# Reordering the first attention layer of a fused attention and FFN kernel: scores behind the values, row maxima turned in a projection bank, normalised rows made on ScalarE

## The chip, the cores and the metric

The kernel runs on one core of a Trainium2 chip. The metric is device time in microseconds of one execution; the result is compared as the median of several runs. The engines are TensorE (PE, with its weight loads as PEld), VectorE (DVE), ScalarE (ACT), GpSimd (POOL) and SyncE (SP), which here only issues DMAs. Each engine carries out its own list of instructions in order; semaphores order them against each other.

## The reference

The program is two transformer-like layers over `x` of 32 batches x 128 rows x 128 columns, with a context of 77 rows per batch. The change touches only the first attention:

```python
x = x + _L0_xattn_ref(_layernorm(x), ctx, ctx, Wq, Wk, Wv, Wo, mask)
# inside: 16 heads of 64, rope on Q and K
Q = (q @ Wq).reshape(b, ql, 16, 64); K = (k @ Wk)...; V = (v @ Wv)...
Q, K = rope(Q), rope(K)
attn = einsum('bqhd,bkhd->bhqk', Q / 8, K)
attn = where(mask == 0, -INF, attn); attn = softmax(attn)
out = einsum('bhqk,bkhd->bqhd', attn, V) @ Wo
```

Then come an FFN, a second attention (16 heads of 8) and a second FFN, each with its layer norm. The mask is given for each batch (128 x 77 int32).

## The kernel before

The first attention goes batch by batch; one batch is a **slot** `b` (0 to 31), two batches are a **pair** `p`, and slot `b` is even (`j == 0`) or odd (`j == 1`) in it. Every engine has a function `slot`, in which its work for a batch is written out by hand; nothing else sets the order. A slot holds work of several batches at once:

- TensorE, for batch `b`: `all_scores` (transposed scores of all heads, 32 small matmuls, L1274, and 16 "fold" matmuls, L1278, which add the mask and subtract each row's maximum), later `values` (L1296), `turn_maxima` (one transpose of the maxima of batch `b + 1`, L1244), `turn_out` (8 transposes of the normalised output, L1307) and `out_projection` (L1316). The fold matmuls read the tile `fold`, which ScalarE copies from the turned maxima (`fold_in`, L1057).
- TensorE, for later batches: `score_maxima(b + 1)` (bf16 scores with the mask, L1223 and L1232, from which VectorE takes each row's maximum, `maxima`, L911), and projections, each three matmuls per piece (`split_product`, L1172 to L1174): four of queries (Q) in each even slot, for the next pair; keys (K tasks, 8 for each group of 4 batches, 308 columns) by the table `KEYS`; values (V, two halves of 512 columns for a tile of 128 context rows) by `VALUE_SLOT`; and the transposes of the next normalised rows (X, L1164, L1167) in each odd slot.
- Rope: VectorE multiplies a projection by the cosines (L845 for Q, L855 for K) and swaps lanes (L848, L858), which frees the projection's bank; GpSimd multiplies the swapped part by the sines and adds (L741 and L742 for Q, L753 and L755 for K). ScalarE casts the results to bf16 (`cast_queries`, L1045; `cast_keys`, L1053), exponentiates the scores (`exps`, L1062 and L1067), copies V out of its bank (`values_in`, L1040) and the turned output (`turned_out`, L1073).
- Layer norm rows: VectorE takes statistics (`statistics`, L806 to L812) in an even slot, GpSimd the power (`pre`, L729), and VectorE in the odd slot makes the mask tile `am` (L801), `kept` (L802), `scale` (L817) and the normalised rows `xhat` (L819).

Two PSUM banks, `pa[0]` and `pa[1]`, take all projections in turn. The list `pa_tasks` names every such task in order; task number `i` uses bank `i % 2`, and TensorE may start it only when task `i - 2` has been read out:

```python
    for i, name in enumerate(pa_tasks()):
        TASK[name] = (i % 2, count[i % 2])
    def empty(engine, name):
        engine.wait_ge(a_free[TASK[name][0]], TASK[name][1])
```

A fourth bank of scores ("S") is one of these tasks; the turned maxima are not, they lie in the score bank `ps[0]`. `cast_keys(b)` waits for all keys that batch `b` may need:

```python
    def keys_of(b):
        return 4 + 4 * (b // 2) if b < 4 else 8 + 8 * (b // 4)
            act.wait_ge(k_roped, keys_roped(keys_of(b)))
```

so batch 2 needs keys 0 to 7, and keys 4 to 7 are made in slot 0. The masks come by DMA into two buffers, `mask_in[p % 2]`; SyncE loads that of pair `p + 2` when the X task of pair `p` has been read.

## Time and profile before

| | us |
|---|---|
| median of 3 runs (717.77 to 719.16) | 718.37 |
| the profiled execution | 719.26 |
| its span in the trace | 716.7 |
| TensorE busy in the span | 680.4 (95%) |
| slots 2 to 31 of the first attention, in the trace | about 64 to 444 |

Times in the trace count from the start of the span. A matmul is drawn with its whole latency, so that neighbours overlap: what it really occupies is the distance from its start to the start of the next. A short wait is therefore not seen as idle time but as a larger distance of two starts.

### The profile page before, as it was taken

How to read it: one execution, taken by the hardware profiler on the slowest of the kernel's cores; microseconds unless marked ns; L12 is line 12 of the kernel's file. 1: busy time of each engine (PE TensorE's matmuls, PEld its weight loads, DVE VectorE, ACT ScalarE, POOL GpSimd, SP SyncE). 2: the span in 40 equal slices, each digit the busy share in tenths (PEclk: the TensorE clock that was granted, in tenths of full speed). 3: DMA queues.
4: the chain of work that ended last, by engine and by line, in shares of the span. 5: the costliest groups of instructions: out<-in, count | busy, mean ns of one | idle time of the engine just before them, and what ended most of it. 6: DMA issues, size and time to landing. Idle time of an engine off the chain costs nothing.

```text
span 716.7 us, 23519 instructions
## 1 busy us (share of the span) xinstructions
PE 680.4 (95%) x9268; PEld 569.8 (80%) x9273; DVE 556.9 (78%) x1635; ACT 388.7 (54%) x846; POOL 432.1 (60%) x558
## 2 busy tenths in 40 slices
PE   8999999999999999999999989999999999998875
PEld 6788888888888888889888878788888888875544
DVE  5887787697687698688687655787878887778996
ACT  2443553543544544445345444566766766766896
POOL 3597586487396388378477523455555646632775
PEclk9999999999999999999999999999999999998999
DMA  9511011101101101101100120000000000000011
GB/s 263 132 34 37 13 48 45 33 5 46 37 26 45 36 2 45 36 26 36 36 22 15 32 79 7 11 7 7 12 5 4 9 4 9 0 2 1 24 45 52
DMA packets 26766, 23.82 MB, mean 33 GB/s; under 512 B 7148, under 2 KB 23356, under 8 KB 26680
## 3 DMA queue, kind: packets, MB, share of 16 engines
q1 hardware_dynamic: 25864, 22.25, 11.1%
q8 instruction: 62, 1.02, 0.6%
q10 hardware_dynamic: 816, 0.36, 0.2%
q14 instruction: 24, 0.20, 0.1%
HBM read 10.25 MB, written 2.10 MB: 17 GB/s over the span
## 4 chain that ended last, share of the span: by engine, by line
PE 70%; DVE 17%; POOL 5%; issue 4%; ACT 3%; DMA 1%; SPq 0%; ACTq 0%; DVEq 0%
PE bank L1274 7%; PE bank L1316 6%; PE bank L1942 6%; PE bank L1172 5%; PE bank L1296 4%; PE bank L1975 4%; PE bank L1278 4%; PE bank L1307 3%; PE bank L1173 3%; PE bank L1174 3%; DVE a_am L911 3%; PE bank L1960 2%; DVE f_h_max L2192 2%; PE bank L1223 2%; PE bank L1232 2%
## 5 line engine op out<-in xcount | busy, mean ns | idle before, releaser
L741 POOL TENSOR_TENSOR a_turned<-a_turned,a_rope 128x512 f32<-128x512 f32 x63 | 81.7, 1297 | 55.7 <-DVE a_turned L848 55.7
L742 POOL TENSOR_TENSOR a_qr<-a_straight,a_turned 128x512 f32<-128x512 f32 x64 | 81.6, 1276 | 4.9
L845 DVE TENSOR_TENSOR a_straight<-bank,a_rope 128x512 f32<-128x512 f32 x63 | 43.0, 683 | 52.5 <-PE bank L1174 51.4
L1045 ACT CAST a_qb<-a_qr 128x512 bf16<-128x512 f32 x64 | 39.8, 622 | 65.9 <-POOL a_qr L742 65.9
L1296 PE MATMUL bank<-a_vs,a_probs 77*64 77x65 f32 x2048 | 66.8, 222 | 0.0
L1296 PEld LDWEIGHTS bank<-a_vs,a_probs 77*64 77x64 f32 x2048 | 62.6, 137 | 3.3
L753 POOL TENSOR_TENSOR a_k_turned<-a_k_turned,a_rope 128x308 f32<-128x308 f32 x61 | 48.4, 793 | 24.3 <-DVE a_k_turned L858 23.6
L1316 PE MATMUL bank<-a_wo,a_oTn 128*128 128x128 f32 x512 | 62.6, 275 | 0.2 <-ACT a_oTn L1073 0.2
L1316 PEld LDWEIGHTS bank<-a_wo,a_oTn 128*128 128x128 f32 x512 | 60.5, 192 | 1.2 <-ACT a_oTn L1073 0.5
L911 DVE TENSOR_REDUCE a_am<-bank 128x6 bf16<-128x462 f32 (+1 forms) x96 | 49.9, 576 | 12.1 <-PE bank L1232 12.0
L1274 PE MATMUL bank<-a_qr,a_kr 64*77 64x128 f32 x960 | 59.2, 273 | 0.0
L1057 ACT COPY a_fold<-bank 112x128 bf16<-112x128 bf16 x32 | 8.5, 266 | 92.4 <-PE bank L1244 92.4
L1067 ACT ACTIVATE a_probs<-bank 77x512 f32<-77x512 f32 x98 | 52.8, 593 | 7.5 <-PE bank L1258 7.5
L1274 PEld LDWEIGHTS bank<-a_qr,a_kr 64*77 64x77 f32 x960 | 52.3, 144 | 5.2 <-issue 5.1
L755 POOL TENSOR_TENSOR a_kr<-a_k_straight,a_k_turned 128x308 f32<-128x308 f32 x62 | 52.0, 840 | 4.8
L848 DVE STREAM_SHUFFLE a_turned<-bank 128x512 f32<-128x512 f32 x63 | 46.3, 735 | 0.0
L1674 DVE TENSOR_REDUCE a_max_m<-bank 128x8 f32<-128x512 f32 x64 | 41.1, 685 | 5.0 <-PE bank L1923 4.6
L1812 ACT ACTIVATE a_qr<-bank 128x512 f32<-128x512 f32 (+1 forms) x96 | 43.8, 536 | 1.0 <-PE bank L1960 1.0
L729 POOL TENSOR_TENSOR a_rstd<-a_var,minus_half 128x2 f32<-128x2 f32 x16 | 11.3, 707 | 51.1 <-DVE a_var L812 51.0
L1073 ACT COPY a_oTn<-bank 128x512 f32<-128x512 f32 x64 | 34.5, 589 | 13.4 <-PE bank L1307 12.8
L1172 PE MATMUL bank<-a_xT_hi,a_wq_hi 128*128 128x256 f32 x128 | 39.9, 312 | 1.3 <-DVE a_wq_lo L939 1.1
L1599 POOL TENSOR_TENSOR a_kr<-a_k_straight,a_blocks 128x128 f32<-128x128 f32 x32 | 12.8, 400 | 46.4 <-ACT a_k_straight L1794 46.4
(282 smaller groups left out, 1984.8 us busy)
## 6 DMA issues: line engine op xcount, KB each, us to landing
a_vs<-a_stage SPq DMA_DIRECT2D x16, 312.8 KB
out<-x_all SPq DMA_DIRECT2D x16, 128.0 KB, 1.8
x_all<-in_x_dram SPq DMA_DIRECT2D x7, 256.0 KB, 6.3
a_vs<-a_stage SPq DMA_DIRECT2D x4, 308.8 KB
a_mask_in<-in_mask SPq DMA_DIRECT2D x16, 77.0 KB, 5.7
a_wv<-in_ctx SPq DMA_DIRECT2D x16, 77.0 KB
a_ctx_in<-in_ctx SPq DMA_DIRECT2D x8, 128.0 KB
a_vs<-a_stage SPq DMA_DIRECT2D x4, 211.2 KB
```

The lines of the kernel that those rows point to most:

```text
L741: steps.link(nc.gpsimd.tensor_tensor(tv, tv, rope[:, 1:2, :].broadcast_to([128, 4, S]), ALU.mult))
L742: nc.gpsimd.tensor_tensor(qr[P][:, 2 * k:2 * k + 2, :, :].rearrange("p t j s -> p (t j) s"), sv, tv, ALU.subtract if made else ALU.add).th ...
L753: steps.link(nc.gpsimd.tensor_tensor(tv, tv, rope[:, 3:4, 0:KL].broadcast_to([128, 4, KL]), ALU.mult))
L755: nc.gpsimd.tensor_tensor(kr[q % 2][:, lo:hi, first:end, :].rearrange("p i j s -> p i (j s)"), view(k_straight[n % 3]), view(k_turned[n % ...
L848: nc.vector.stream_shuffle(turned[k % 3][:], pv, mask=[lane ^ 1 for lane in range(32)]).then_inc(a_free[TASK["Q", p, k][0]], 1)
L911: nc.vector.tensor_reduce(rows, ps[bk][:, 0:n * KL].rearrange("p (h k) -> p h k", k=KL), AX, ALU.max).then_inc(s_free[bk], 1)
L1067: nc.scalar.activation(probs[:, 4 * g:4 * g + 4, :], ps[ST_BANK[g]][0:KL, :].rearrange("p (h s) -> p h s", s=S), ACT.Exp).then_inc(s_free[ ...
L1172: nc.tensor.matmul(out, lhs_hi, rhs_hi, start=True, stop=False)
L1274: nc.tensor.matmul(banks[g][0:KL, i * S:(i + 1) * S], kr[b // 4 % 2][e:e + 64, h // 2, b % 4, :], qr[P][e:e + 64, h // 2, j, :], start=i = ...
L1296: last = nc.tensor.matmul(po[r][rows, VW * i:VW * (i + 1)], probs[:, PROBS_SLOT[h], rows], vs[b % RING][:, h, :], start=True, stop=True)
L1316: last = nc.tensor.matmul(po[2][:, 0:D], oTn[:, i, :], wo[:, i, :], start=i == 0, stop=i == TILES - 1)
L1812: nc.scalar.activation(probs[:, 4 * g:4 * g + n, :], SCORES[g].rearrange("p (t s) -> p t s", s=S), ACT.Exp).then_inc(s_free[g], 1)
```

## The change

What each engine does in a slot is written in a new order, for slots 0 to 29; slots 30 and 31 keep theirs.

- TensorE: `all_scores(b + 1)` (only the 32 score matmuls) is issued directly behind `values(b)`, then `turn_maxima(b + 1)`, then `turn_out(b)`. The 16 fold matmuls of `all_scores` become `all_folds`, the first thing of the next slot.
- The turned maxima are a task of their own ("T") in the two projection banks, ahead of "S" in the list.
- Keys and values are spread otherwise over the slots: keys `lead` come directly behind the folds; an even slot from 4 to 26 has one key there (before, its one or two keys stood behind the score maxima and behind the values), an odd slot `4q + 1` six (before five).
- ScalarE makes the normalised rows (two passes over two batches, in the even slot), which VectorE made in the odd slot; GpSimd makes `scale`; VectorE gets `kept` straight from `mask_in`, in `statistics` of the even slot.
- ScalarE casts the keys of `b + 1` and of `b + 2` in the even slot (before, those of `b + 1` in each slot) and the queries two and two; `turned_out(b)` moves to the end of slot `b`.
- SyncE loads the mask of a pair when `am` of the pair before last has been made.

The core of the diff (lines as long as they are; "..." where left out):

```diff
-    VALUE_SLOT = {8 * o + s: VT * o + i for o in range(B // 8) for i, s in enumerate((-3, 0 if o == 0 else -1, 1, 3, 4))
-                  if 8 * o + s >= 0}
+    VALUE_SLOT = {0: (1,), **{8 * o + 1: (VT * o + 2,) for o in range(B // 8)}, **{8 * o + 3: (VT * o + 3,) for o in range(B // 8)},
+                  **{8 * o + 5: (VT * o + 4,) for o in range(B // 8)},
+                  **{8 * o - 1: (VT * o, VT * o + 1) for o in range(1, B // 8)}}
...
-    KEYS, LATE_KEYS = {0: range(4, 8), 1: range(8, 11), 2: range(14, 16)}, {1: range(11, 14)}
+    KEYS = {0: ((), (), range(4, 6), range(6, 8)), 1: (range(8, 9), range(9, 10), range(10, 12), range(12, 14)),
+            2: (range(14, 16), (), (), ())}
     for q in range(1, B // 4 - 1):
         n = 8 + 8 * q
-        KEYS[4 * q], KEYS[4 * q + 1], LATE_KEYS[4 * q + 1] = range(n, n + 2), range(n + 2, n + 5), range(n + 5, n + 7)
-        KEYS[4 * q + 2] = range(n + 7, n + 8)
...
+        KEYS[4 * q] = (range(n, n + 1), (), (), ())
+        KEYS[4 * q + 1] = (range(n + 1, n + 2), range(n + 2, n + 3), range(n + 3, n + 5), range(n + 5, n + 7))
+        KEYS[4 * q + 2] = (range(n + 7, n + 8), (), (), ())
...
+                    + [("V", 0, 1), ("C",), ("X", 1), ("T", 0), ("S", 0)])
...
+                yield from lead + queries[:2] + middle + queries[2:3] + first_half + second_half + queries[3:] + late
             else:
-                yield from values[:1] + rows + values[1:]
+                rows = [("X", p + 2)] if p + 2 < PAIRS else []
+                yield from lead + first_half + second + second_half + middle + later_first + rows + later_second + late
+            if b + 1 < B - 2:
+                yield "T", b + 1
+                yield "S", b + 1
...
-            if j == 0 and more_pre(p):
-
-                read(sp, ("X", p))
-                load_mask(p + 2)
+            if b == 0 or j == 1 and more_pre(p + 1):
+                at = 0 if j == 0 else p + 1
+                sp.wait_ge(masks_made, at + 1)
+                load_mask(at + 2)
...
+            steps.link(nc.gpsimd.tensor_tensor(rstd[p % 2][:], var[p % 2][:], t["minus_half"][:, 0:2], ALU.pow))
+            nc.gpsimd.tensor_tensor(scale[:], kept[p % 2][:], rstd[p % 2][:], ALU.mult).then_inc(rstd_ready, 1)
...
+            if p > 1:
+                dve.wait_ge(xhat_ready, p)
+                dve.wait_ge(masks_in[p % 2], 16 * (p // 2) + 16)
+                steps.link(nc.vector.tensor_reduce(kept[p % 2][:], mask_in[p % 2][:], AX, ALU.max, apply_absolute_value=True))
+                steps.did(nc.vector.tensor_scalar(kept[p % 2][:], kept[p % 2][:], 0.5, -1.0, ALU.is_ge, ALU.mult))
...
+        def normalised_rows(p):
+            act.wait_ge(rstd_ready, p + 1)
+            for j in range(2):
+                nc.scalar.activation(xhat[:, j, :], x[:, 2 * p + j, :], ACT.Identity, bias=mv[p % 2][:, j, 0:1],
+                                     scale=-1.0).then_inc(rows_centred, 1)
+            for j in range(2):
+                act.wait_ge(rows_centred, 2 * (p - 2) + j + 1)
+                last = nc.scalar.activation(xhat[:, j, :], xhat[:, j, :], ACT.Identity, scale=scale[:, j:j + 1])
+            last.then_inc(xhat_ready, 1)
...
+            if b < B - 2:
+                nc.scalar.copy(fold[:], full(act, ("T", b))[:].bitcast(BF16)[0:FOLD, 0:S]).then_inc(a_free[TASK["T", b][0]], 1)
+                return
...
+            else:
+                exps(b, (3, 0, 1, 2))
+                if j == 0:
+                    if more_pre(p):
+                        normalised_rows(p + 2)
+                    cast_keys(b + 1)
+                    cast_queries(p + 1, 1 - P, 0)
+                    for u in ahead_values(b):
+                        values_in(u, 0)
+                        values_in(u, 1)
+                    cast_keys(b + 2)
+                    cast_queries(p + 1, 1 - P, 1)
+                else:
+                    for u in ahead_values(b):
+                        values_in(u, 0)
+                        if later_values(b):
+                            values_in(u, 1)
+                    cast_queries(p + 1, 1 - P, 2)
                     cast_queries(p + 1, 1 - P, 3)
-                    cast_keys(b + 1)
-                if more_pre(p) and ahead:
-                    transposed(("X", p + 2))
-                if u is not None and not ahead:
-                    values_in(u, 0)
-                if more_pre(p) and not ahead:
-                    transposed(("X", p + 2))
-                if more:
-                    fold_in(b + 1)
-                if u is not None:
-                    if ahead:
+                    for u in ahead_values(b):
+                        if not later_values(b):
+                            values_in(u, 1)
+                    for u in later_values(b):
                         values_in(u, 0)
-                    values_in(u, 1)
-                if last_pair(p):
-                    next(second)
+                    if more_pre(p):
+                        transposed(("X", p + 2))
+                    for u in later_values(b):
+                        values_in(u, 1)
+                fold_in(b + 1)
+                if b + 1 < B - 2:
+                    turned_out(b, 0)
+                    turned_out(b, 1)
...
+        def all_folds(b):
+            pe.wait_ge(a_free[TASK["T", b][0]], TASK["T", b][1] + 1)
+            banks = (ps[0], ps[1], ps[2], pa[TASK["S", b][0]])
...
+        all_scores(0, 0, 0)
...
-                all_scores(b, P, j)
+                all_folds(b)
+                for n in lead:
+                    project_keys(n)
                 if first:
                     pe.wait_ge(keys_split, 2)
                 project_queries(p + 1, (0, 1))
-                for n in middle_keys(b):
+                for n in middle:
                     project_keys(n)
                 if not first:
                     out_projection(b - 1)
                 project_queries(p + 1, (2,))
+                for u in ahead_values(b):
+                    project_values(u, 0)
                 score_maxima(b + 1, P, 1)
-                for n in even_keys(b)[:-1]:
+                for u in ahead_values(b):
+                    project_values(u, 1)
+                project_queries(p + 1, (3,))
+                for n in late:
                     project_keys(n)
-                project_queries(p + 1, (3,))
                 for r in range(3):
                     values(b, P, j, r)
+                all_scores(b + 1, P, 1)
                 turn_maxima(b + 1, P, 1)
-                if u is not None:
-                    project_values(u, 0)
-                    project_values(u, 1)
-                for n in even_keys(b)[-1:]:
-                    project_keys(n)
+                turn_out(b)
...
-                all_scores(b, P, j)
-                turn_out(b - 1)
-                for n in ahead:
+                all_folds(b)
+                for n in lead:
                     project_keys(n)
-                if u is not None and not ahead:
+                for u in ahead_values(b):
                     project_values(u, 0)
+                for n in second_keys:
+                    project_keys(n)
+                if not lead:
+                    for u in ahead_values(b):
+                        project_values(u, 1)
                 out_projection(b - 1)
+                if lead:
+                    for u in ahead_values(b):
+                        project_values(u, 1)
+                for n in middle:
+                    project_keys(n)
+                for u in later_values(b):
+                    project_values(u, 0)
                 if more_pre(p):
                     transposes(("X", p + 2))
-                for n in behind:
+                score_maxima(b + 1, 1 - P, 0)
+                for u in later_values(b):
+                    project_values(u, 1)
+                for n in late:
                     project_keys(n)
-                score_maxima(b + 1, 1 - P, 0)
                 for r in range(3):
                     values(b, P, j, r)
+                if b + 1 < B - 2:
+                    all_scores(b + 1, 1 - P, 0)
                 turn_maxima(b + 1, 1 - P, 0)
-                if u is not None:
-                    if ahead:
-                        project_values(u, 0)
-                    project_values(u, 1)
-                for n in late_keys(b):
-                    project_keys(n)
                 turn_out(b)
```

Where it moves instructions, as the compiled programs list them.

VectorE at the start of slot 0, before (`a0_` marks the first attention, `masks_in0` is the semaphore of the mask DMA of even pairs; the four rope instructions of the next pair's first queries come last):

```order
L806 BN_STATS a0_st6<-x_all 128x6 [waits a0_x_in]
L806 BN_STATS a0_st6<-x_all 128x6
L808 MEMSET a0_var0 128x2 [waits a0_dve_step]
L810 BN_AGGR a0_mv0<-a0_st6 128x2 x2
L812 TENSOR_SCALAR a0_var0<-a0_mv0 128x2 [waits a0_dve_step]
L845 TENSOR_TENSOR a0_straight<-bank0,a0_rope 128x512 [waits a0_roped,a0_a_full0]
L848 STREAM_SHUFFLE a0_turned<-bank0 128x512
```

and of the change:

```order
L810 TENSOR_REDUCE a0_kept0<-a0_mask_in0 128x2 [waits a0_masks_in0,a0_xhat_ready,a0_x_in]
L811 TENSOR_SCALAR a0_kept0<-a0_kept0 128x2 [waits a0_dve_step]
L813 BN_STATS a0_st6<-x_all 128x6 x2
L815 MEMSET a0_var0 128x2 [waits a0_dve_step]
L817 BN_AGGR a0_mv0<-a0_st6 128x2 x2
L819 TENSOR_SCALAR a0_var0<-a0_mv0 128x2 [waits a0_dve_step]
L852 TENSOR_TENSOR a0_straight<-bank1,a0_rope 128x512 [waits a0_roped,a0_a_full1]
```

Two instructions that wait for the mask of pair 2 now stand ahead of the statistics and of the queries' rope; before, the first reader of that mask was L801 in slot 1.

ScalarE in slot 0, from the exponentials of batch 0 to the fold copy of batch 1, before (`kb` the cast keys, `qb` the cast queries, `a0_k_roped` counts keys finished by GpSimd):

```order
L1067 ACTIVATE a0_probs<-bank4 77x512 [waits a0_s_full2]
L1045 CAST a0_qb<-a0_qr1 128x512 [waits a0_roped]
L1057 COPY a0_fold<-bank2 112x128 [waits a0_s_full0]
L1045 CAST a0_qb<-a0_qr1 128x512 [waits a0_roped]
L1040 COPY a0_stage<-bank1 128x8x64 [waits a0_a_full1]
L1040 COPY a0_stage<-bank0 128x8x64 [waits a0_a_full0]
```

and of the change:

```order
L1086 ACTIVATE a0_probs<-bank4 77x512 [waits a0_s_full2]
L1032 ACTIVATE a0_xhat<-x_all,a0_mv0 128x128 [waits a0_rstd_ready]
L1032 ACTIVATE a0_xhat<-x_all,a0_mv0 128x128
L1036 ACTIVATE a0_xhat<-a0_xhat,a0_scale 128x128 [waits a0_rows_centred] x2
L1069 CAST a0_kb1<-a0_kr0 128x616 [waits a0_a_free1,a0_a_free0,a0_k_roped]
L1061 CAST a0_qb<-a0_qr1 128x512 [waits a0_roped]
L1056 COPY a0_stage<-bank0 128x8x64 [waits a0_a_full0]
L1056 COPY a0_stage<-bank1 128x8x64 [waits a0_a_full1]
L1069 CAST a0_kb0<-a0_kr0 128x616 [waits a0_a_free1,a0_a_free0,a0_k_roped]
L1061 CAST a0_qb<-a0_qr1 128x512 [waits a0_roped]
L1073 COPY a0_fold<-bank1 112x128 [waits a0_a_full1]
```

The second key cast, of batch 2, has come ahead of the fold copy of batch 1; before, it stood in slot 1, behind all exponentials of batch 1.

TensorE from the values of batch 7 into slot 8, before:

```order
L1296 MATMUL bank<-a_vs,a_probs 64x65 x32
L1244 MATMUL bank<-identb,a_am 112x128
L1172 MATMUL bank<-a_wv_hi,a_ctxT_hi 128x512
L1173 MATMUL bank<-a_wv_lo,a_ctxT_hi 128x512
L1174 MATMUL bank<-a_wv_hi,a_ctxT_lo 128x512
L1307 MATMUL bank<-ident,a_out_n 128x128 x8
L1274 MATMUL bank<-a_qr,a_kr 77x128 x16
L1278 MATMUL bank<-a_fold,a_fold_w 77x128 x16
L1172 MATMUL bank<-a_xT_hi,a_wq_hi 128x256
L1173 MATMUL bank<-a_xT_lo,a_wq_hi 128x256
L1174 MATMUL bank<-a_xT_hi,a_wq_lo 128x256
```

and of the change:

```order
L1322 MATMUL bank<-a_vs,a_probs 64x65 x32
L1296 MATMUL bank<-a_qr,a_kr 77x128 x16
L1263 MATMUL bank<-identb,a_am 112x128
L1333 MATMUL bank<-ident,a_out_n 128x128 x8
L1304 MATMUL bank<-a_fold,a_fold_w 77x128 x16
L1188 MATMUL bank<-a_ctxT_hi,a_wk_hi 128x308
L1189 MATMUL bank<-a_ctxT_lo,a_wk_hi 128x308
L1190 MATMUL bank<-a_ctxT_hi,a_wk_lo 128x308
L1188 MATMUL bank<-a_xT_hi,a_wq_hi 128x256
L1189 MATMUL bank<-a_xT_lo,a_wq_hi 128x256
L1190 MATMUL bank<-a_xT_hi,a_wq_lo 128x256
```

The scores follow the values without a transpose or a projection between, the output's transposes stand between the turned maxima and the folds, and a key projection stands ahead of the two first query projections. With T, S, K, Q0, Q1 as successive tasks, Q1 has the bank of K.

## Rows read from the trace of the kernel before

**Rows 1.** The page, part 1: busy us (share) of each engine.
```profile
PE 680.4 (95%) x9268; PEld 569.8 (80%) x9273; DVE 556.9 (78%) x1635; ACT 388.7 (54%) x846; POOL 432.1 (60%) x558
```
**Rows 2.** Windows: length, each engine's busy us, TensorE's clock, DMA share, GB/s.
```profile
33.00:64.00 31.00, 28.35 (x365) 24.20 (x365) 24.50 (x70) 12.57 (x25) 24.75 (x27) 1.00 0.16 44
64.00:444.00 380.00, 369.81 (x5283) 323.51 (x5282) 288.40 (x767) 176.25 (x358) 240.11 (x250) 1.00 0.11 32
```
**Rows 3.** Waits of PE from 64 to 444: us in total, times, longest.
```profile
PE bank L1307 <- DVE a_out_n L918: 2.1, 7, 0.7
```
**Rows 4.** Tile `a_mask_in` from 28 to 40: issue, and time to landing.
```profile
L658 SPq DMA_DIRECT2D a_mask_in<-in_mask x1: 544/544/544, 28.8 to 28.8; - x1
...
DMA to landing us min/median/max: 8.6/8.6/8.6
```
**Rows 5.** Timeline of DVE in slot 0: start, us, instruction, idle before.
```profile
30.37 0.48 DVE L806 BATCH_NORM_STATS2 a_st<-x_all 128x6 f32<-128x128 f32 x2
...
31.17 0.17 DVE L812 TENSOR_SCALAR a_var<-a_mv 128x2 f32<-128x2 f32 x1
33.80 0.69 DVE L845 TENSOR_TENSOR a_straight<-bank,a_rope 128x512 f32<-128x512 f32 x1 [2.46 <-PE bank L1174]
```
**Rows 6.** Source L802, all its instances: ns min/median/max.
```profile
L802 DVE TENSOR_REDUCE a_kept<-a_am x16: 313/314/316, 5.2 to 388.4; 128x2 f32<-128x154 bf16 x16
```
**Rows 7.** Timeline of POOL: first query and last key of slot 0.
```profile
35.22 1.28 POOL L741 TENSOR_TENSOR a_turned<-a_turned,a_rope 128x512 f32<-128x512 f32 x1 [3.09 <-DVE a_turned L848]
...
51.57 0.84 POOL L755 TENSOR_TENSOR a_kr<-a_k_straight,a_k_turned 128x308 f32<-128x308 f32 x1
```
**Rows 8.** Timeline of ACT in slots 0 and 1.
```profile
43.13 0.27 ACT L1057 COPY a_fold<-bank 112x128 bf16<-112x128 bf16 x1 [4.63 <-PE bank L1244]
43.30 0.62 ACT L1045 CAST a_qb<-a_qr 128x512 bf16<-128x512 f32 x1
...
52.44 0.71 ACT L1053 CAST a_kb<-a_kr 128x616 bf16<-128x616 f32 x1 [1.01 <-POOL a_kr L755]
```
**Rows 9.** Timeline of PE: key 4 of slot 0, and the folds of batches 1 and 2.
```profile
35.28 0.31 PE L1172 MATMUL bank<-a_ctxT_hi,a_wk_hi 128*128 128x154 f32 x1 [0.81 <-DVE a_turned L848]
...
47.32 1.09 PE L1278 MATMUL bank<-a_fold,a_fold_w 112*77 112x128 bf16 x16
...
63.85 1.09 PE L1278 MATMUL bank<-a_fold,a_fold_w 112*77 112x128 bf16 x16
```
**Rows 10.** Timeline of PE, slot 1: a value half and three keys in alternating banks.
```profile
57.02 0.47 PE L1172 MATMUL bank<-a_wv_hi,a_ctxT_hi 128*128 128x512 f32 x1
...
58.72 0.38 PE L1172 MATMUL bank<-a_ctxT_hi,a_wk_hi 128*128 128x308 f32 x1
...
59.42 0.38 PE L1172 MATMUL bank<-a_ctxT_hi,a_wk_hi 128*128 128x308 f32 x1
...
60.47 0.38 PE L1172 MATMUL bank<-a_ctxT_hi,a_wk_hi 128*128 128x308 f32 x1 [0.39 <-DVE a_k_turned L858]
```
**Rows 11.** Windows around the one fall of TensorE's clock.
```profile
658.00:660.00 2.00, 0.11 (x2) 0.06 (x2) 1.93 (x9) 0.62 (x1) 0.86 (x2) 0.81 0.00 0
660.00:662.00 2.00, 2.00 (x6) 0.72 (x7) 2.00 (x6) 1.10 (x2) 1.85 (x3) 0.50 0.01 4
...
666.00:668.00 2.00, 1.65 (x15) 1.37 (x14) 1.93 (x5) 0.90 (x2) 0.33 (x1) 0.98 0.00 0
```
**Rows 12.** Timeline of PE, slot 8: a key, a query, values.
```profile
147.28 0.38 PE L1172 MATMUL bank<-a_ctxT_hi,a_wk_hi 128*128 128x308 f32 x1
...
147.78 0.34 PE L1172 MATMUL bank<-a_xT_hi,a_wq_hi 128*128 128x256 f32 x1
...
148.31 0.28 PE L1173 MATMUL bank<-a_xT_lo,a_wq_hi 128*128 128x256 f32 x1
148.43 0.28 PE L1174 MATMUL bank<-a_xT_hi,a_wq_lo 128*128 128x256 f32 x1
148.64 2.09 PE L1296 MATMUL bank<-a_vs,a_probs 77*64 77x65 f32 x64
```

More of the change, by code:

```diff
@@ L527, in pa_tasks @@
-            ahead, behind = odd_keys(b)
-            rows = [("X", p + 2)] if p + 2 < PAIRS else []
-            if ahead:
-                yield from tasks(ahead) + rows + tasks(behind) + values + tasks(late_keys(b))
-            else:
-                yield from values[:1] + rows + values[1:]
+            p = b // 2
+            lead, second, middle, late = ([("K", n) for n in some] for some in keys_at(b))
+            first_half, second_half = ([("V", u, half) for u in ahead_values(b)] for half in range(2))
@@ L776, in slot @@
                     rope_turn(p + 1, 1 - P, 2)
[L777 to L779 removed]
                     rope_turn(p + 1, 1 - P, 3)
[L781 removed]
+                for n in late:
                     rope_keys(n)
             else:
[L784 to L785 removed]
+                for n in (*lead, *second_keys, *middle, *late):
                     rope_keys(n)
@@ L1005, in slot @@
                     next(second)
+                if more_pre(p) and lead:
+                    split_turned(("X", p + 2))
                 if more:
                     maxima(b + 1, 1 - P, 0)
-                if more_pre(p) and not ahead:
+                if more_pre(p) and not lead:
                     split_turned(("X", p + 2))
+                for n in late:
+                    rope_keys(n)
                 normalise(b)
```

141 lines of the change are left out of this document (57 added, 84 removed).

## The prediction

> **What bounds the kernel now.** I read the page's first part, then the windows of the first attention, its waits, and the timelines of the start engine by engine. TensorE is busy 95% of the span, VectorE 78% [rows 1]. From 64 to 444, slots 2 to 31, TensorE shows 380.0 - 369.8 = 10.2 us of idle time [rows 2], of several kinds; the largest, 2.1, is that of the output's transposes, which wait for VectorE's normalised output [rows 3]. A matmul's drawn tail hides the start of each wait, so the true sum is larger: the key at 60.47 shows 0.39 idle, but the key before it (start 59.42) was through at 59.92, since a key unhindered takes 147.78 - 147.28 = 0.50 [rows 12], so that the wait is 0.54 [rows 10]. I estimate 13.6 us for the stage. TensorE is the bound there, and no reordering can give more than these waits. In the start it is different: the stretch from 33 to 64 has 2.65 us of idle TensorE [rows 2], and GpSimd works from 35.22 to 52.41 without a pause [rows 7] through four queries and four keys.
>
> **The start, slot 0.** Two edits put something slow ahead of something urgent.
>
> First, VectorE now reads the mask of pair 2 before it does anything else in slot 0. That mask's DMA was issued at 28.8 and landed 8.6 us later, at 37.4 [rows 4]. Its issue does not move: SyncE is busy with earlier loads and places values until then, and both versions' conditions are met by that time. VectorE was ready for its statistics at 30.37 [rows 5]. From 30.37 to the end of L812, 31.34, the statistics take 0.97; the reduce adds 0.31 [rows 6], the small operation about 0.2 (like L812, 0.17). So the rope of the first query starts at 37.4 + 0.97 + 0.5 = 38.9, with the wake-up 39.0, instead of 33.80 [rows 5]: 5.2 us late. 2.46 us of VectorE's time before 33.80 were idle, and that is the only cover. The first waiter behind it is TensorE: key 4 needs the bank of that query, and starts at 40.5 instead of 35.28 [rows 9]. GpSimd starts its first query at 40.4 instead of 35.22, and its run of 52.41 - 35.22 = 17.2 us, now with keys 6 and 7 as the last, ends at 57.6 [rows 7]. A price of another kind stands in the Trainium skill, DMA: Bandwidth & Descriptors, section Anatomy of one DMA: a fixed cost of about 2.0 us and little for so small a transfer. By that page the mask would be there at about 31, VectorE would wait under 1 us inside its idle gap, and the whole 5.2 would be nothing; no load here supports it, this one took 8.6.
>
> Second, ScalarE casts the keys of batch 2 ahead of the fold copy of batch 1. The cast waits for key 7, the last thing GpSimd makes in slot 0. In the kernel before it waited as well, until 52.44, but behind the exponentials of batch 1 [rows 8]. Behind it now stand a query cast and the fold copy: 57.65 + 0.61 + 0.5 + 0.25 = 59.0 (drawn 0.71, 0.62 and 0.27, but back to back each gives way about 0.1 earlier, as 43.13 to 43.30 shows) [rows 8], and the folds of batch 1 start at 59.15. What is queued behind this one copy is everything: the folds are TensorE's next instruction, and all engines feed on it. TensorE would be ready earlier: 40.5 + (47.32 - 35.28) [rows 9] + 0.8 for the transposes of the output (already done by then) = 53.3. So it stands idle twice, about 5.8 us after the second query and 5.8 us ahead of the folds.
>
> Against 47.32 [rows 9] the folds of batch 1 are 11.8 us late, 0.8 of it work done ahead: **+11.0 us**. Small losses (the fold copy now also lies bare ahead of the folds of batch 0, 0.5 us) vanish inside the mask wait.
>
> **Slot 1.** Before, from folds to folds, 63.85 - 47.32 = 16.5 us [rows 9], of which I read 2.1 as waits. The new order has 1.5 (below): **-0.6**.
>
> **Slots 2 to 29.** What it removes: the output's transposes now have 1.9 us of scores ahead of them, the turned maxima too, and the rows are ready a slot earlier. The 13.6 us go. What it adds are bank waits, because the two projection banks alternate strictly. The price of a short turn: a key's bank comes free for its second successor 60.47 - 58.72 = 1.75 us after the key's start, a value half's 58.72 - 57.02 = 1.70 [rows 10]; VectorE was free in the first case, so this is the least.
> - An even slot with one leading key: K (0.51), Q0 (0.77: six steps of 0.12 and a first one longer by 0.05), then Q1 in K's bank. Ready after 1.28 [rows 12], allowed after 1.75: 0.47, and with the exposed weight load 0.55. Twelve slots: 6.6. Slot 2 with two leading keys: 0.9.
> - An odd slot 4q + 1, six keys: the second key waits for the first behind one value half (0.46), the third in its run for the value half (0.42 + 0.07), the rows' transposes for a key (0.33), the last key for the rows, which ScalarE and VectorE read one after the other (0.27). Sum 1.55; six such slots after slot 1: 9.3.
> - An odd slot 4q + 3: nothing; everything it needs is ready.
>
> Sum 16.8 against 13.6: **+3.2**. Moved off VectorE: the normalised rows, 26 instructions in this stage; they were ahead of its rope and are worth nothing beyond the waits already counted. On ScalarE they add four short activations per pair on an engine 46% busy (176.25 of 380) [rows 2]; the nearest row, a copy of 0.27 [rows 8], gives 1.1 us, behind exponentials and ahead of casts with over 1 us to spare. If that cover failed it would cost up to 1.1 in each even slot, 15 us in all; I take nothing.
>
> Changes of array shape: from whole-array products to the values 148.43 to 148.64 is 0.21 where the step before is 0.12 [rows 12]: 0.09 for each change. Scores directly behind values save one or two of three changes, about 0.09 per slot in 28 slots, 2.5; in nine odd slots a projection now separates score maxima and values, 0.8 back: **-1.7**. The bounds are 0 and twice that.
>
> **TensorE's clock.** It fell once, in the window from 658, where TensorE was busy 0.11 of 2 us, and stayed at 1.2 of 2.4 GHz for about 0.8 + 6 + 0.1 = 6.8 us [rows 11]. The new idle stretches are longer than that one. The first is followed by 5.8 us of slack, which swallows the slow stretch and so shortens the second. If the clock falls again in the second, dense work at half rate loses up to 3.4. I take **+1.0**, bounds 0 and 4. The Trainium skill (TensorE: Matmul & The Clock Gate, section HAM oscillation) says that long waits of TensorE are paid again as slow matmuls, which speaks against the change in the same sense.
>
> **Sum.** 11.0 - 0.6 + 3.2 - 1.7 + 1.0 = +12.9. The profiled execution took 719.26; 732.2 as such an execution, and since the median of the runs was 0.9 below it, 731.3.
>
> **Rivals.**
> - The mask comes early (chance 0.12). The two waits of slot 0 are in series only through VectorE. If the mask lands by 31.5, only the key cast counts: 52.8 + 1.5 = 54.35 for the folds, +6.2 instead of +11.0, and 726.5. For it: other mask loads landed sooner. Against: the one at that very time took 8.6, behind context and value transfers that are still issued with it [rows 4]. The fixed price of the Trainium skill's DMA page, above, would give this case.
> - The bank waits do not appear (0.08), so that the reordering does what it could: faster. The place is the leading key of the even slots and the six keys; it decides when the new waits of slots 2 to 29 sum to less than 4 instead of 16.8. With none: 719.26 + 11.0 - 0.6 - 13.6 - 1.7 = 714.4, median 713.5. For it: 13.6 us of waits are really removed. Against: 1.75 us for a bank is measured, and the start's loss must be paid first.
> - More is lost (0.12): ScalarE, one queue with rows, casts, folds and output copies, is late for the folds in steady slots, or the clock falls twice. At 0.3 us in each of 28 slots, or 3.4 + 1 for the clock: 737 to 741.
> - The forecast, both waits in slot 0 and a steady stage about as before: 0.68, in a range of its own from 726 to 736.
>
> **How the numbers follow.** The time is that of the forecast. Taking the early mask and half of "more is lost" gives 722 to 738, with a tenth left on either side. A measurement of this kernel tells 0.2% (1.4 us) from no change. Faster takes the rival of missing bank waits, 0.07, no change 0.03 for a mix of it with an early mask, slower 0.90.
>
> **What would show it.** In the trace of the change: VectorE's reduce over `a_mask_in` at about 37.5, with idle ahead of it put down to the DMA; the second key cast of slot 0 at about 57.6, waiting for GpSimd, and the folds of batch 1 near 59; TensorE's clock below full in a window between 38 and 66; a wait of about 0.2 to 0.3 drawn on the second query of even slots for VectorE's `a_k_turned`; no wait of L1307's successor for `a_out_n`. Wrong would be: the mask landing before 32, the key cast before 53, or even slots clearly under 12.2 us from folds to folds with the key in front.

## The result, and the profile of the changed kernel

The changed kernel takes 727.03 us (median of 4 runs, 725.17 to 729.35), the kernel before 718.76 beside it (4 runs, 717.77 to 719.58). The ratio is 1.0117, with an interval of 1.0084 to 1.015: 8.3 us slower. Forecast were 731.3 and a range of 722 to 738. The profiled execution was the fastest of the four: 725.17 us, span 723.4, which is 5.9 and 6.7 above the one shown before. The last experiment bears on the difference between +8.3 and +5.9.

The page's first part, as in [rows 1]; VectorE has 29 us less of busy time, ScalarE and GpSimd have 12 and 3 more:

```profile
PE 683.8 (95%) x9268; PEld 573.9 (79%) x9273; DVE 528.0 (73%) x1607; ACT 400.9 (55%) x902; POOL 435.0 (60%) x572
```

The windows of [rows 2] again. From 33 to 64 TensorE's busy time has gone from 28.35 to 23.86, from 64 to 444 it has grown by 2:

```profile
33.00:64.00 31.00, 23.86 (x232) 19.70 (x231) 16.69 (x53) 11.38 (x24) 21.01 (x23) 0.89 0.10 28
64.00:444.00 380.00, 372.03 (x5314) 326.01 (x5313) 265.44 (x753) 186.55 (x406) 245.19 (x265) 1.00 0.12 33
```

Slot 0, engine by engine. VectorE waits for the mask (answers to [rows 5]), and the rope of the first query follows at 36.41 instead of 33.80:

```profile
35.10 0.31 DVE L810 TENSOR_REDUCE a_kept<-a_mask_in 128x2 f32<-128x154 int32 x1 [5.18 <-DMA a_mask_in<-in_mask]
...
36.41 0.69 DVE L852 TENSOR_TENSOR a_straight<-bank,a_rope 128x512 f32<-128x512 f32 x1
```

The mask itself was issued at 27.7 and landed 7.2 later (answers to [rows 4]):

```profile
L655 SPq DMA_DIRECT2D a_mask_in<-in_mask x1: 544/544/544, 27.7 to 27.7; - x1
...
DMA to landing us min/median/max: 7.2/7.2/7.2
```

ScalarE stands in front of the second key cast until GpSimd has finished key 7 (54.02 + 0.83), with the fold copy two places behind (answers to [rows 8]):

```profile
54.89 0.70 ACT L1069 CAST a_kb<-a_kr 128x616 bf16<-128x616 f32 x1 [8.13 <-POOL a_kr L756]
55.50 0.61 ACT L1061 CAST a_qb<-a_qr 128x512 bf16<-128x512 f32 x1
56.02 0.26 ACT L1073 COPY a_fold<-bank 112x128 bf16<-112x128 bf16 x1
```

And TensorE pays twice, ahead of key 4 and ahead of the folds of batch 1. They start at 37.89 and 56.33, where the kernel before had them at 35.28 and 47.32 [rows 9]:

```profile
37.89 0.31 PE L1188 MATMUL bank<-a_ctxT_hi,a_wk_hi 128*128 128x154 f32 x1 [3.50 <-DVE a_turned L855]
...
56.33 1.09 PE L1304 MATMUL bank<-a_fold,a_fold_w 112*77 112x128 bf16 x16 [2.08 <-ACT a_fold L1073]
```

TensorE's clock, in the windows of its two waits: it fell after the first one, and stayed up through the second.

```profile
38.00:40.00 2.00, 1.69 (x10) 1.52 (x11) 1.76 (x6) 1.47 (x4) 1.92 (x2) 0.64 0.00 0
40.00:42.00 2.00, 2.00 (x11) 2.00 (x11) 0.92 (x3) 0.62 (x1) 1.92 (x3) 0.50 0.00 0
...
54.00:56.00 2.00, 0.24 (x3) 0.01 (x1) 0.00 (x0) 1.11 (x2) 0.83 (x1) 1.00 0.00 0
```

The rest is best read from the starts of the folds, one slot after another. This table is worked out from the traces, and e1 to e8 are the experiments below: the first row from the folds of batch 0 to those of batch 2, the second from there to those of batch 30 (28 slots, 2 to 29). After slot 29 the distance between the two kernels stays at 6.4 to 6.7.

| us, from the traces | before | after | e1 | e2 | e3 | e4 | e5 | e6 | e7 | e8 |
|---|---|---|---|---|---|---|---|---|---|---|
| slots 0 and 1 | 31.95 | 39.55 | 39.17 | 37.66 | 32.40 | 33.42 | 32.77 | 37.69 | 32.40 | 43.57 |
| slots 2 to 29 | 358.91 | 357.77 | 357.80 | 357.78 | 357.69 | 351.49 | 354.19 | 392.75 | 349.56 | 357.67 |
| slot 4, one key (before and e7: two) | 13.69 | 12.78 | 12.79 | 12.78 | 12.76 | 12.26 | 12.24 | 13.76 | 12.67 | 12.79 |
| slot 5, six keys (before and e7: five) | 14.82 | 15.03 | 15.02 | 15.02 | 15.03 | 15.03 | 15.50 | 16.56 | 14.27 | 15.02 |

The whole loss lies in slots 0 and 1, +7.6; the 28 steady slots are 1.1 faster.

### The profile page after: what moved, and what is told of

Same layout as the page of the kernel before. It is cut to its first block, busy times and chain, and to the rows that moved or that the text cites. A ratio compares the mean times of both kernels' runs of the same rounds, so it can differ in the third digit from the quotient of the medians.

```text
span 723.4 us, 23623 instructions
## 1 busy us (share of the span) xinstructions
PE 683.8 (95%) x9268; PEld 573.9 (79%) x9273; DVE 528.0 (73%) x1607; ACT 400.9 (55%) x902; POOL 435.0 (60%) x572
## 4 chain that ended last, share of the span: by engine, by line
PE 78%; DVE 8%; issue 4%; SPq 3%; POOL 3%; ACT 3%; DMA 1%; ACTq 0%; DVEq 0%
PE bank L1322 8%; PE bank L1342 8%; PE bank L1296 7%; PE bank L1981 6%; PE bank L1188 5%; PE bank L2014 4%; PE bank L1333 4%; PE bank L1304 4%; PE bank L1190 3%; PE bank L1189 3%; PE bank L1999 2%; PE bank L1239 2%; DVE f_h_max L2231 2%; PE bank L1250 2%; PE bank L1955 1%
## 5 line engine op out<-in xcount | busy, mean ns | idle before, releaser
L862 DVE TENSOR_TENSOR a_k_straight<-bank,a_rope 128x308 f32<-128x308 f32 x61 | 28.9, 474 | 48.3 <-PE bank L1190 47.5
L1086 ACT ACTIVATE a_probs<-bank 77x512 f32<-77x512 f32 x98 | 51.3, 602 | 7.5 <-PE bank L1280 7.5
L1188 PE MATMUL bank<-a_xT_hi,a_wq_hi 128*128 128x256 f32 x128 | 41.6, 325 | 2.8 <-issue 0.7
L936 DVE TENSOR_TENSOR x_all<-bank,x_all 128x128 f32<-128x128 f32 x32 | 9.3, 292 | 44.4 <-PE bank L1342 44.2
```

Of the source, the lines that this page charges most:

```text
L1086: nc.scalar.activation(probs[:, 4 * g:4 * g + 4, :], ps[ST_BANK[g]][0:KL, :].rearrange("p (h s) -> p h s", s=S), ACT.Exp).then_inc(s_free[ ...
L1188: nc.tensor.matmul(out, lhs_hi, rhs_hi, start=True, stop=False)
```

## The experiments

The first four kernels were run on one chip against 15 runs of the kernel before (median 719.02), the other four on another chip against 9 (719.27). So a difference in us between e4 and one of e5 to e7 is one between chips; the slot lengths of the table and the ratios bear it out.

**e1_mask.** The mask of pair 2 is loaded earlier; the cast stays.

```diff
+        sp.wait_ge(masks_made, 1)
+        load_mask(2)
...
-            if b == 0 or j == 1 and more_pre(p + 1):
-                at = 0 if j == 0 else p + 1
+            if j == 1 and more_pre(p + 1):
+                at = p + 1
```

> The mask of pair 2 is issued ahead of the later loads of the start, as soon as VectorE has used up the mask of pair 0, with the same waits otherwise; the cast of batch 2's keys stays where the change put it. Theory A (the time is lost in slot 0, to two waits, and the steady slots only break even): VectorE's reduce over a_mask_in starts at about 30 instead of 35.1 and draws no idle time, TensorE's first idle stretch in slot 0 is gone and with it the fall of its clock near 38, key 7 is ready on GpSimd at about 52 instead of 54.9, and the folds of batch 1 start at about 53.5 instead of 56.3; the span falls by 2 to 3.5 us against the changed kernel. Rival B (the new bank waits of slots 2 to 29 make the time, the start is made good later): the span falls by less than 1 us. Rival C (the loads that are now behind the mask's, context and values, are themselves urgent): another wait for a DMA takes its place on TensorE or ScalarE before 40 us, and nothing is gained or up to 2 us lost.

Measured: 723.74 us (5 runs, 723.59 to 724.86), ratio 1.0068 (1.0054 to 1.0082). VectorE's reduce starts at 29.96 with no idle time, key 4 at 35.31 as in [rows 9]. The folds of batch 1 start at 53.76, and now the clock falls in front of them:

```profile
53.76 1.29 PE L1306 MATMUL bank<-a_fold,a_fold_w 112*77 112x128 bf16 x10 [4.30 <-ACT a_fold L1075]
```

```profile
52.00:53.00 1.00, 0.00 (x0) 0.00 (x0) 0.00 (x0) 0.68 (x2) 0.29 (x1) 1.00 0.00 0
53.00:54.00 1.00, 0.24 (x3) 0.24 (x4) 0.00 (x0) 1.00 (x4) 0.00 (x0) 0.54 0.00 0
54.00:55.00 1.00, 1.00 (x12) 1.00 (x11) 0.00 (x0) 1.00 (x3) 0.00 (x0) 0.50 0.00 0
```

The second wait stands here alone: 4.30 instead of 2.08, because nothing ahead of it made TensorE late. The slow stretch then falls on dense work: slot 1 takes 17.34 instead of 15.04. So of the 2.57 by which the folds start earlier, 2.3 are given back in this execution, the slowest of the five: its span is 723.1, only 0.3 below that of the changed kernel's fastest. The medians differ by 3.3, within the expected 2 to 3.5; that the clock would fall at the other wait no theory had. Rival C did not appear. Rival B has its sign, under 1 us of span, but not its reason: slots 2 to 29 are the same.

**e2_cast.** The cast of batch 2's keys is moved behind the query casts of slot 1; the mask stays late.

```diff
-                    cast_keys(b + 2)
+                    if b > 0:
+                        cast_keys(b + 2)
...
                     cast_queries(p + 1, 1 - P, 3)
+                    if b == 1:
+                        cast_keys(2)
```

> Only the cast of batch 2's keys is moved, from slot 0, where it stands ahead of the copy of batch 1's folds, to the end of ScalarE's work in slot 1; the mask of pair 2 is late as in the changed kernel. Theory A: ScalarE's fold copy for batch 1 no longer waits for key 7 on GpSimd, and the folds of batch 1 start as soon as TensorE is through with the projections of slot 0, at about 53 instead of 56.3; the second idle stretch (54 to 56) is gone; the span falls by 2 to 3.5 us, and the slow stretch of the clock stays as it is, since its end near 46 lies before. Rival C (the copy of the folds is in fact late behind a query's cast, whose query GpSimd makes just before key 7): the fold copy then waits for that, and the gain is under 1 us. Rival B: under 1 us, the start is made good later.

Measured: 722.99 us (5 runs, 722.56 to 724.34), ratio 1.0056 (1.0043 to 1.007): 4.0 below the changed kernel. The wait ahead of the folds is gone, they start at 54.73; the mask wait is there, longer than before, since the mask landed at 35.9 in this execution:

```profile
36.05 0.32 DVE L810 TENSOR_REDUCE a_kept<-a_mask_in 128x2 f32<-128x154 int32 x1 [5.86 <-DMA a_mask_in<-in_mask]
```

Rival C fell: the fold copy now waits only for TensorE, whose turned maxima it copies.

```profile
54.05 0.27 ACT L1073 COPY a_fold<-bank 112x128 bf16<-112x128 bf16 x1 [6.11 <-PE bank L1266]
```

TensorE's clock fell behind the wait for the mask here too, and this time no slack follows:

```profile
38.84 0.47 PE L1191 MATMUL bank<-a_ctxT_hi,a_wk_hi 128*128 128x154 f32 x1 [4.19 <-DVE a_turned L855]
```

From this key to the folds of batch 1 TensorE takes 15.89; in e3, at full clock, it takes 13.99.

**e3_both.** Both edits.

> Both edits together, nothing else. Theory A: the two waits are in series, so that their removal adds up to nearly all of the 8.2 us that slot 0 lost: folds of batch 1 at 48 to 49 instead of 56.3 (46.5 is the least, since one batch of transposed output, 0.8, is already done by then), span 6.5 to 8.5 us below the changed kernel and within 1.5 us of the kernel before. The steady slots keep their length: 12.8 for an even slot with a key in front, 15.0 for an odd one with six keys. Rival B: a gain of under 3 us, and the kernel stays over 4 us above the one before, the rest lying in slots 2 to 29. Rival D (the rows normalised on ScalarE are ready later than before, and delay the next projection in slot 1 once the waits ahead are gone): slot 1 grows from 15.0 by 2 us or more.

Measured: 718.82 us (11 runs, 717.97 to 719.22), ratio 0.9998 (0.9989 to 1.0007). Span 716.5, 6.9 below the changed kernel's. The folds of batches 1 and 2:

```profile
49.68 1.06 PE L1309 MATMUL bank<-a_fold,a_fold_w 112*77 112x128 bf16 x16
...
64.71 0.50 PE L1309 MATMUL bank<-a_fold,a_fold_w 112*77 112x128 bf16 x6
```

The folds of batch 1 are 0.7 us later than the expected 48 to 49, and slot 1 is 15.03, so rival D fell. The two edits give 3.3 and 4.0 alone and 8.2 together; in the traces of e1 and e2 each edit alone leaves one wait with a fall of the clock behind it, and e3 has neither. Theory A holds: the two waits of slot 0 are the loss, and all the rest of the change is worth nothing in sum.

**e4_both_key.** As e3, and the key in front of the queries of the even slots goes behind the output's projection, on all three engines.

```diff
-        KEYS[4 * q] = (range(n, n + 1), (), (), ())
+        KEYS[4 * q] = ((), (), range(n, n + 1), ())
...
-        KEYS[4 * q + 2] = (range(n + 7, n + 8), (), (), ())
+        KEYS[4 * q + 2] = ((), (), range(n + 7, n + 8), ())
...
-                for n in middle:
-                    project_keys(n)
                 if not first:
                     out_projection(b - 1)
+                for n in middle:
+                    project_keys(n)
```

> As e3_both, and in the even slots the one leading key (batches 4, 8, ... and 6, 10, ...) is moved from ahead of the queries to behind the second query and the output's projection, on TensorE, VectorE and GpSimd alike. Theory A with its price of a short bank turn (the second query waits for the bank of the key ahead of it, 0.3 to 0.55 us a slot, twelve slots): even slots with a key shrink from 12.8 to 12.3 to 12.5 from folds to folds, and the span falls by a further 4 to 6 us, so that the kernel is faster than the one before by 0.4 to 0.9%. Rival E (the wait only moves: the query behind the key then waits for the key's bank, or the next query's turned rows come later): even slots stay at 12.7 to 12.9 and the time is that of e3_both within 1 us. Rival F (the key behind the second query delays GpSimd's third query and so the maxima and the casts): slots grow, and the time is above that of e3_both.

Measured: 712.36 us (4 runs, 711.68 to 713.23), ratio 0.9907 (0.9892 to 0.9922), 6.5 below e3 (expected were 4 to 6). First the changed kernel in slot 6: the second query (125.96) waits for the bank of the key (124.30). From the last step but one of the first query (125.45) it is 0.51 where two steps are 0.24:

```profile
124.30 0.39 PE L1188 MATMUL bank<-a_ctxT_hi,a_wk_hi 128*128 128x308 f32 x1
...
125.45 0.28 PE L1189 MATMUL bank<-a_xT_lo,a_wq_hi 128*128 128x256 f32 x1
...
125.96 0.38 PE L1188 MATMUL bank<-a_xT_hi,a_wq_hi 128*128 128x256 f32 x1
```

Then e4, folds of batches 6 and 7: 12.25 apart instead of 12.78.

```profile
117.15 1.06 PE L1309 MATMUL bank<-a_fold,a_fold_w 112*77 112x128 bf16 x16
...
129.40 0.67 PE L1309 MATMUL bank<-a_fold,a_fold_w 112*77 112x128 bf16 x9
```

All twelve such slots shrink by 0.50 to 0.54 against e3, 6.2 in sum (357.69 to 351.49), and nothing of it comes back: rivals E and F fell. In this execution the clock also fell in slot 0, where the program is that of e3. Slot 0 took 18.40 instead of 17.37:

```profile
36.00:37.00 1.00, 0.64 (x6) 0.52 (x6) 1.00 (x5) 0.45 (x1) 0.92 (x2) 1.00 0.07 21
37.00:38.00 1.00, 1.00 (x8) 1.00 (x8) 0.74 (x3) 0.00 (x0) 1.00 (x1) 0.79 0.01 4
38.00:40.00 2.00, 2.00 (x9) 1.58 (x7) 1.47 (x6) 0.62 (x1) 1.92 (x3) 0.50 0.00 0
```

Two of the four runs, this one among them, took 713.0 and 713.2 at a granted clock of 0.994, the other two 711.7 at 0.998, so that this fall seems to come in some executions only; the other three have no trace.

**e5_rows_dve.** As e4, with the rows of the pairs from 2 on normalised on VectorE (the second piece is ScalarE's slot).

```diff
                     masks(p + 2, P)
+                    normalised_rows(p + 2)
                 residual(b - 1)
...
-                    if more_pre(p):
-                        normalised_rows(p + 2)
```

> As e4_both_key, but the normalised rows of the pairs from 2 on are made by VectorE again, in the odd slots behind the mask's values, as in the kernel before (one operation of 128x512 a batch in place of two activations on ScalarE); the masked scale is unchanged. Theory A (TensorE is the bound in the steady slots, VectorE is busy 73% and has room; that the rows went to ScalarE is worth nothing by itself, as the prediction took it): every slot keeps its length within 0.05 us and the time is that of e4_both_key within 1 us. Rival G (the odd slots with six keys hang on VectorE, which frees the banks): the residual and the two middle keys' ropes start about 1.2 us later, so that those six slots grow by 0.5 to 1 us each, 3 to 6 us in all. Rival H (ScalarE was in fact late): the time falls by over 1 us.

Measured: 715.03 us (4 runs, 714.63 to 715.32), ratio 0.9943 (0.9927 to 0.9958), so 2.7 slower than e4. Rival G is right in kind, its size a little under the 0.5 to 1 it gave: the six-key slots from slot 5 on grow by 0.43 to 0.48 each, slot 1 by 0.39, all others are unchanged to 0.03. VectorE is busy, and the banks come free later:

```profile
105.52 0.77 DVE L803 TENSOR_SCALAR a_am<-a_mask_in 128x154 bf16<-128x154 int32 x1
106.22 1.78 DVE L829 SCALAR_TENSOR_TENSOR a_xhat<-x_all,a_mv,a_scale 128x128 f32<-128x128 f32 x2
107.92 0.28 DVE L939 TENSOR_TENSOR x_all<-bank,x_all 128x128 f32<-128x128 f32 x1
108.13 0.46 DVE L865 TENSOR_TENSOR a_k_straight<-bank,a_rope 128x308 f32<-128x308 f32 x1
```

TensorE's waits between 64 and 430 have a first line that e4 has not, the transposes of the rows:

```profile
PE bank L1185 <- DVE a_k_turned L868: 3.3, 6, 0.6
```

**e6_out_first.** As e4, but the next batch's scores stand behind the output's transposes.

```diff
-                all_scores(b + 1, P, 1)
                 turn_maxima(b + 1, P, 1)
                 turn_out(b)
...
             elif j == 0:
+                if not first:
+                    all_scores(b, P, 0)
                 all_folds(b)
```

> As e4_both_key, but TensorE makes the next batch's scores behind the transposes of the output and directly ahead of their folds, instead of directly behind the values; nothing else moves. Theory A (the scores are the cover of VectorE's normalisation of the output, and this is where most of the removed waits lay): the transposes of the output wait for VectorE in nearly every slot, about 0.6 to 1.2 us, which makes 28 slots longer by 0.5 to 1.1 and the kernel slower by 14 to 30 us; the idle time before the transposes is put down to a_out_n. The fold copy then has the scores as its cover, so that nothing else is lost. Rival I (the turned maxima and the exponentials' banks give enough time, or the normalisation is short): under 3 us slower.

Measured: 757.98 us (4 runs, 757.11 to 759.84), ratio 1.0535 (1.0519 to 1.0551), 45.6 above e4. The steady slots with keys grow by 1.5, those without by 1.0 to 1.3. TensorE's longest wait from 64 to 470, and one of its 29 instances with the clock around it:

```profile
PE bank L1338 <- DVE a_out_n L927: 31.1, 29, 1.2
```

```profile
181.95 1.97 PE L1338 MATMUL bank<-ident,a_out_n 128*128 128x128 f32 x8 [1.21 <-DVE a_out_n L927]
```

```profile
182.00:184.00 2.00, 2.00 (x10) 1.67 (x12) 1.91 (x8) 0.63 (x2) 1.35 (x2) 0.50 0.07 19
```

The direction of theory A is right and its size too small, 14 to 30 us against 45.6. The wait is drawn with 0.67 to 1.22, 31.1 in 29 slots, and the slots grow by about 0.3 more than that. The clock fell in slots 9 and 13, behind such waits of 1.2, and these took 18.06 and 18.18 where slots 5, 17 and 21 take 16.6. It fell in slot 1 in the same way, and in slot 0 with no wait of over 0.81 ahead of it, as in e4.

**e7_five.** As e4, with five keys in the odd slots and two in the even slot ahead.

```diff
-        KEYS[4 * q] = ((), (), range(n, n + 1), ())
-        KEYS[4 * q + 1] = (range(n + 1, n + 2), range(n + 2, n + 3), range(n + 3, n + 5), range(n + 5, n + 7))
+        KEYS[4 * q] = ((), (), range(n, n + 1), range(n + 1, n + 2))
+        KEYS[4 * q + 1] = (range(n + 2, n + 3), range(n + 3, n + 4), range(n + 4, n + 5), range(n + 5, n + 7))
```

> As e4_both_key, but one of the six keys of the odd slots 5, 9, 13, ... 25 is moved to the even slot ahead, behind the fourth query, so that this even slot has two keys and the odd one five. Theory A (an odd slot's waits are those for projection banks at 1.7 to 1.75 us after the start of the instruction group that used the bank before): the key behind the output's projection that waited for the value half's bank is gone with its 0.49, but the rows' transposes take its place in the same bank and wait about 0.4; the even slots grow by one key without a wait, 0.50, the odd ones shrink by 0.7 to 0.9. Net 0.2 to 0.4 in each of six pairs of slots, 1.2 to 2.4 us in all. Rival J (the late key in the even slot is in the way of the normalisation on VectorE, or GpSimd is late with it and the folds' casts wait): the even slots grow by over 0.7 and the time is equal or above.

Measured: 710.15 us (4 runs, 709.75 to 710.85), ratio 0.9874 (0.9859 to 0.9889): the fastest version here, 9.1 us below the kernel before. Even slots 4q grow by 0.42, the odd ones shrink by 0.75, 0.33 net in each of six pairs, as expected. (Slots 0 and 1 take what they take in e3, with the clock up.)

**e8_filled.** The changed kernel with 40 matmuls on an idle tile in slot 0, ahead of key 4.

```diff
                 project_queries(p + 1, (0, 1))
+                if first:
+                    idle_products(40)
```

> The changed kernel itself with one addition: 40 matmuls on an idle tile (0.107 us each in the start, 4.3 us together) stand on TensorE in slot 0 behind the second query's projection, where it waits for the bank that VectorE holds while the mask of pair 2 is late; both waits of slot 0 remain. Theory A (the slow stretch of the clock from 38.6 to 45.4 lies ahead of a wait of 3.5 us and is swallowed by it): the slow stretch there is gone, TensorE waits longer in front of the folds of batch 1 instead (over 5 us), and these start at the same time, 56.3, within 0.3; if the clock stays up, the time is that of the fastest runs of the changed kernel. Rival K (the longer wait in front of the folds makes the clock fall there instead, as it did in e1_mask): the folds start at 56.3, but slot 1 takes 17.3 instead of 15.0, and the time is 2 us above. Rival L (the slow stretch did cost time ahead of the folds): they start 1 to 3 us earlier.

Measured: 728.04 us (5 runs, 725.79 to 729.4), ratio 1.0117 (1.0101 to 1.0132), the same as the changed kernel. The slow stretch near 40 is gone, and comes at the folds of batch 1 instead, so that slot 1 takes 17.16; rival K is right in this:

```profile
38.00:40.00 2.00, 1.02 (x11) 0.70 (x8) 1.92 (x9) 0.33 (x2) 1.01 (x3) 1.00 0.00 0
...
58.00:60.00 2.00, 1.56 (x15) 1.56 (x16) 0.00 (x0) 2.00 (x6) 0.00 (x0) 0.50 0.00 0
```

But the folds start at 58.44, later than any theory said, and the reason is upstream:

```profile
37.18 0.31 DVE L810 TENSOR_REDUCE a_kept<-a_mask_in 128x2 f32<-128x154 int32 x1 [7.05 <-DMA a_mask_in<-in_mask]
...
38.48 0.69 DVE L852 TENSOR_TENSOR a_straight<-bank,a_rope 128x512 f32<-128x512 f32 x1
```

The same load, behind the same transfers, landed at 37.1 here, at 35.9 in e2 and at 34.9 in the changed kernel's trace. From the first rope to the folds of batch 1 it is 19.96 here and 19.92 in the changed kernel (36.41 to 56.33): the slow stretch that only the latter has in between cost nothing there, and rival L fell.

## Why the prediction was right, point by point

- **Mask wait, right.** VectorE's reduce over `a_mask_in` stands there with 5.18 idle. Forecast was a landing at 37.4, from the one load of [rows 4]; the trace had 34.9, other executions 35.9 and 37.1. "Its issue does not move" was wrong by 1.1 us (27.7 instead of 28.8), and the time to landing is 7.2 to 8.6, of which the forecast had only the 8.6. The first rope started at 36.41 instead of 39.0, key 7 was ready at 54.85 instead of 57.6. So the rival of the early mask did not come. The Trainium skill (DMA: Bandwidth & Descriptors, Anatomy of one DMA — SWDGE (gpsimd) path) gives its fixed cost of about 2.0 us for loads issued from GpSimd. This one is issued by SyncE, among other transfers, and took 7.2 to 8.6, so the prediction should not have priced the rival with it.
- **Key cast, right.** The order on ScalarE, the wait for GpSimd and the 1.5 us from key 7 to the folds came as forecast: 54.85 to 56.33 is 1.48.
- **The term +11.0 was mis-sized.** Measured were 9.01 - 0.80 = 8.2 in the profiled execution (0.80 for the transposes of the output done ahead). Of the error of 2.8, 2.6 is the mask's: the first rope was forecast at 39.0 and came at 36.41. In e8, with the mask at 37.1, the folds start at 58.44, forecast 59.15. The forecast was one end of a spread that one trace cannot show.
- **Slot 1, -0.6.** 16.53 to 15.04 is -1.49, of which 0.80 is the transposes done ahead: -0.69.
- **Slots 2 to 29, +3.2 and -1.7.** Forecast +1.5, measured -1.1. The price of a short bank turn held: the second query stands 1.66 after the key's start (forecast 1.75), and taking the key away gave 0.52 a slot in e4 (forecast 0.55 with twelve slots, 6.6; measured 6.2). Of the waits for `a_out_n`, 2.1 us in seven places before [rows 3], one of 0.7 is left. The wait on the second query was to be drawn with 0.2 to 0.3; nothing is drawn there, it shows only in the starts. The four waits forecast for a six-key slot can be read from the starts of slot 5 in the changed kernel's trace:

```profile
109.27 0.39 PE L1188 MATMUL bank<-a_ctxT_hi,a_wk_hi 128*128 128x308 f32 x1
...
111.03 0.38 PE L1188 MATMUL bank<-a_ctxT_hi,a_wk_hi 128*128 128x308 f32 x1 [0.24 <-DVE a_k_turned L865]
...
113.23 0.48 PE L1188 MATMUL bank<-a_wv_hi,a_ctxT_hi 128*104 128x512 f32 x1
...
114.01 0.31 PE L1188 MATMUL bank<-a_ctxT_hi,a_wk_hi 128*128 128x308 f32 x1
...
114.94 0.38 PE L1188 MATMUL bank<-a_ctxT_hi,a_wk_hi 128*128 128x308 f32 x1 [0.34 <-ACT a_stage L1056]
...
115.69 0.41 PE L1180 MATMUL bank<-ident,a_xhat 128*128 128x128 f32 x2
...
117.30 0.38 PE L1188 MATMUL bank<-a_ctxT_hi,a_wk_hi 128*128 128x308 f32 x1
...
117.94 0.38 PE L1188 MATMUL bank<-a_ctxT_hi,a_wk_hi 128*128 128x308 f32 x1
```

The banks turn after 1.76 (109.27 to 111.03), 1.71 and 1.68. Less what TensorE does in between (a key 0.50, or 0.43 behind a value half; a value half 0.78), the waits are about 0.48, 0.50, 0.25 and 0.14, 1.37 instead of 1.55. As an estimate from these starts, the six-key slots are 1.1 below their term, the leading keys 0.4 (6.2 instead of 6.6) and slot 2 0.15 (its two keys and the wait take 1.75, 0.75 of it wait, forecast 0.9). That is about 1.6 of the 2.6 us: the new waits were over-counted. The last 1.0 lies in the estimate of the waits removed (13.6) or of the changes of array shape (1.7, bounds 0 and 3.4); no run separates these two, and it stays open.
- **Rows off VectorE, "worth nothing beyond the waits already counted".** Too bold. In the new order they are worth 0.46 in each six-key slot, 2.7 us by slots 2 to 29 and by the medians of e4 and e5 (ratios 0.9907 and 0.9943, whose intervals don't touch); back on VectorE the rows stand ahead of the ropes that free the banks. The forecast's 16.8 was worked out with VectorE free, so that these 2.7 do not come on top of it: they are the price of that condition.
- **Clock, +1.0.** 0 in the profiled execution, since the fall came ahead of slack, as e8 shows. e1 and e8 show what the second case costs, 2.1 to 2.3 in slot 1, within the bounds of 0 and 4 that the prediction gave. Over the four runs the granted clock was 0.993, 0.988, 0.991 and 0.991; the profiled one is the 0.993. A later mask and a fall ahead of slot 1 would account for the 2 us between it and the median; since the other three have no trace, that is argued, not shown.
- **The rival "more is lost".** Its 737 to 741 counts the clock's +1.0 twice and starts from 732.2 instead of 731.3; with the forecast's own base it is 735 to 740. It did not come.

## What to carry to other kernels

A reordering that is sound in every steady slot can lose in its first one: look there for each in-order queue where something slow (a load, the last product of the slowest engine) now stands ahead of something urgent, and price that place on its own. Two small moves, one load and one cast, took back all 8.2 us. Between tasks that alternate in two banks, write down the start distances: a short task behind a short task waits, and moving it behind a long one (the output's projection, 1.70 us) was worth 0.5 us in each of twelve slots. And take the landing time of a load in a crowded stretch from several executions, or plan with its late end.

## What the runs showed that was not expected

- The landing time of one load (the mask of pair 2, 77 KB, beside other transfers) varied between executions of the same loads from 7.2 to 8.6 us, and its issue from 27.7 to 28.8.
- TensorE's clock fell from 2.4 to 1.2 GHz after waits of 4.30 (e1), 4.19 (e2), 4.34 (e8) and 3.50 us, and stayed up through one of 2.08. But it also fell with no long wait at all: in slot 0 of e4 at about 37.5, with TensorE busy 0.64 of the us ahead of it, where e3 ran the same instructions at full clock, and in slots 1, 9 and 13 of e6 behind a wait of 1.2 that more than ten other slots passed at full clock.
- What a fall costs depends on what follows it: nothing ahead of slack (the changed kernel, slot 0), 1.0 us in slot 0 of e4, 1.9 in slot 0 of e2, 1.5 in e6, 2.1 to 2.3 ahead of dense work (e1, e8). The Trainium skill (TensorE: Matmul & The Clock Gate, HAM oscillation) tells of waits for a DMA that are paid again as slow matmuls. The long waits of e1, e2 and e8 agree; behind the one of the changed kernel's slot 0 the matmuls were slow too, but no time was paid.
